# Cross-attention of a fused decoder layer: order of the probability scaling, steps that make the keys, slot of the context split

## The reference, cut to what matters

```python
x = _layernorm(x + _L0_attn_ref(x, ...))
x = _layernorm(x + _L0_xattn_ref(x, ctx_1024, ctx_1024, Wq, Wk, Wv, Wo))
x = _layernorm(x + _L0_ffn_ref(x, ...))
# _L0_xattn_ref: 32 sequences, 256 queries of width 256, 120 context rows, 16 heads of 64
q = jnp.einsum('bsd,dhk->bshk', query_input, Wq)
k = jnp.einsum('bsd,dhk->bshk', key_input, Wk)
v = jnp.einsum('bsd,dhk->bshk', value_input, Wv)
logits = jnp.einsum('bthk,bfhk->bhft', k, q * depth ** (-0.5))
ctx = jnp.einsum('bhft,bthk->bfhk', jax.nn.softmax(logits, axis=-1), v)
return jnp.einsum('bfhk,hkd->bfd', ctx, Wo)
```

## Time and profile before

| what | value |
|---|---|
| median of 3 runs | 3204.7 us |
| profiled execution | 3207.9 us |
| its span | 3206.2 us |
| cross-attention, first to last `shift` (L1275, 256 steps) | 1218.6 to 2302.8 us of the span |
| busy in 1300 to 2253 us (953 us): PE, PEld, DVE, ACT, POOL | 909.05, 861.73, 850.67, 836.25, 586.65 us |

### The profile page before, as it was taken

One profiled execution on the slowest core, in us unless ns is written; L12 is line 12 of the kernel. 1 busy time (PEld: TensorE's weight loads), 2 busy tenths in 40 slices (PEclk: granted clock), 3 DMA queues, 4 the chain that ended last, 5 costly groups with the idle time before them and its releaser, 6 DMA issues. The chain is left out here.

```text
span 3206.2 us, 79485 instructions
## 1 busy us (share of the span) xinstructions
PE 3067.2 (96%) x22112; PEld 2854.9 (89%) x22112; DVE 2376.3 (74%) x6822; ACT 2245.6 (70%) x7186; POOL 1874.9 (58%) x3414
## 2 busy tenths in 40 slices
PE   6999999999999988999999999999779999999998
PEld 5999999999999988998999988899768888889998
DVE  5787777777877777888889889898745455554565
ACT  6888888888887777888888888888734444442222
POOL 3666767666776766666666656666636666653000
PEclk8999999999999999999999999999889999999999
DMA  6444444444444440211111111111234444433333
GB/s 179 116 124 126 125 123 123 120 121 125 110 122 120 120 126 24 64 44 54 54 45 53 57 44 60 48 48 57 81 109 112 107 97 100 111 73 80 124 124 105
DMA packets 193705, 300.82 MB, mean 94 GB/s; under 512 B 33856, under 2 KB 134080, under 8 KB 192704
## 3 DMA queue, kind: packets, MB, share of 16 engines
q1 hardware_dynamic: 168768, 262.91, 27.7%
q0 software_dynamic: 24576, 33.57, 6.2%
HBM read 116.02 MB, written 67.11 MB: 57 GB/s over the span
## 5 line engine op out<-in xcount | busy, mean ns | idle before, releaser
L973 POOL TENSOR_SCALAR ca_prob<-ca_prob,ca_inverse 128x120 f32<-128x120 f32 x1024 | 360.5, 371 | 221.8 <-DVE ca_inverse L1281 219.5
L665 ACT ACTIVATE sa_prob<-sa_prob,sa_shift 128x128 f32<-128x128 f32 (+1 forms) x1024 | 453.7, 461 | 2.6 <-DVE sa_shift L718 2.6
L1218 ACT ACTIVATE ca_prob<-bank,ca_shift 128x120 f32<-128x120 f32 x1024 | 353.9, 362 | 18.8 <-DVE ca_shift L1275 17.4
L460 POOL TENSOR_SCALAR sa_prob<-sa_prob,sa_inverse 128x128 f32<-128x128 f32 x512 | 200.2, 391 | 231.0 <-DVE sa_inverse L726 217.1
L718 DVE CUSTOM_DVE_ANT_0 sa_prob<-bank,sa_mask 128x128 f32<-128x128 f32 (+1 forms) x1024 | 304.6, 352 | 6.2 <-PE bank L138 2.2
L136 PE MATMUL bank<-sa_ow,sa_y_hi 128*128 128x256 f32 x1024 | 278.8, 303 | 0.0
L136 PE MATMUL bank<-sa_kvT_a,sa_q 128*128 128x128 f32 (+1 forms) x1024 | 250.6, 280 | 18.1 <-DMA sa_q<-sa_q_tile 17.6
L138 PE MATMUL bank<-sa_kvT_b,sa_q 112*128 112x128 f32 (+1 forms) x1024 | 261.1, 280 | 0.0
L749 DVE TENSOR_TENSOR sa_pT_lo<-bank,sa_pT_hi 128x384 fp32r<-128x384 f32 x512 | 258.3, 544 | 1.5 <-ACT sa_pT_hi L650 1.4
L138 PE MATMUL bank<-sa_ow,sa_y_lo 112*128 112x256 f32 x1024 | 258.0, 282 | 0.0
L1694 POOL DMA_INDIRECT mid_acc<-ex_out,ex_to_tokens x112 | 191.0, 1705 | 105.4 <-DVE ex_out L1956 73.1
(11 more groups left out here) (257 smaller groups left out, 12179.8 us busy)
## 6 DMA issues: line engine op xcount, KB each, us to landing
sa_q<-sa_q_tile SPq DMA_DIRECT2D x128, 288.0 KB
sa_q<-sa_q_tile SPq DMA_DIRECT2D x160, 112.0 KB
mid_x2T<-ca_x2T SPq DMA_DIRECT2D x32, 512.0 KB
ex_sx<-mid_x2T SPq DMA_DIRECT2D x32, 512.0 KB
sa_q<-sa_q_tile SPq DMA_DIRECT2D x304, 32.0 KB, 2.0
sa_xT_raw<-in_xT SPq DMA_DIRECT2D x32, 256.0 KB, 2.9
sa_q<-sa_q_tile SPq DMA_DIRECT2D x32, 256.0 KB
sa_x_res<-in_x SPq DMA_DIRECT2D x32, 256.0 KB
```

What stands on the lines that cost most here:

```text
L460: pool.tensor_scalar(prob[:, r, hh, 0:P], prob[:, r, hh, 0:P], inverse[:, r, 2 * hh:2 * hh + 1], 1.0, ALU.mult, ALU.mult)
L665: act.activation(prob[:, r, hh, cols], prob[:, r, hh, cols], ACT.Exp, bias=shift[:, r, n:n + 1], scale=-1.0, accum_out=total[:, r, n:n + 1 ...
L973: ins = pool.tensor_scalar(prob[:, r, t, hh], prob[:, r, t, hh], inverse[:, r, n:n + 1], 1.0, ALU.mult, ALU.mult)
L1218: act.activation(prob[:, r, t, hh], SC[g % 2][:, n * S:n * S + S], ACT.Exp, bias=shift[:, r, n:n + 1], accum_out=total[:, r, n:n + 1]).the ...
```

## The change

Three edits, all in the cross-attention.

1. On GpSimd the scaling of step m-5 comes before the context split of step m-9.
2. The keys of pair pr are no longer made in its steps 0 to 7 but in the steps K_AT = -4, -3, -1, 0, 2, 3, 5, 6 counted from its first, so in slots 14 and 15 of the pair before and 1, 2, 4, 5, 7, 8 of its own. Pair 0 keeps steps 0 to 7. Functions `k_step`, `k_at` and `keys_by` say which key a step makes and how many are made by then; TensorE now waits in every slot until the keys so far have been read from the shared bank.
3. The context tile of a pair is split four slots ahead (CT_AT = -4, slot 12 of the pair before).

The loop over bodies ends one body earlier; body 7 is written out, since its last steps make no keys. The words "halved value products" answer to no line of the diff: the four matmuls of lines 1088 and 1089 are as they were.

```diff
+    def k_step(J, pr, p):
+        return p if isinstance(J, int) and J == 0 and pr == 0 else pr * 2 * NP + K_AT[p]
+    def pairs_near(J, g):
+        return [pr for pr in range(g // (2 * NP), g // (2 * NP) + 2)
+                if pr >= 0 and (not isinstance(J, int) or J * (SEQS // 2) + pr < B // 2)]
+    def k_at(J, g):
+        return next(((pr, p) for pr in pairs_near(J, g) for p in range(NP) if k_step(J, pr, p) == g), None)
+    def keys_by(J, g):
+        done = sum(k_step(J, pr, p) <= g for pr in range(4) for p in range(NP) if not isinstance(J, int) or J * (SEQS // 2) + pr < B // 2)
+        return J * (SEQS // 2 * NP) + done
+    def pair_at(J, m):
+        at = 0 if isinstance(J, int) and J == 0 and m == 0 else CT_AT
+        pr = (m - at) // (2 * NP)
+        here = (m - at) % (2 * NP) == 0 and seq_exists(J, 2 * pr) and not (isinstance(J, int) and J == 0 and pr == 0 and m != 0)
+        return pr if here else None
...
+    K_AT, CT_AT = (-4, -3, -1, 0, 2, 3, 5, 6), -4
...
 gpsimd:
-            g = m - CL - 1
-            (c_hi, c_lo)
             g = m - IL
             (prob by inverse, four operations)
+            g = m - CL - 1
+            (c_hi, c_lo)
...
 tensor:
-                if b == 1 and p == 0:
-                    need(pe, klo_done, upto_pair(J, g // (2 * NP), NP))
-                if b == 0:
-                    need(pe, clo_done, upto_pair(J, g // (2 * NP)))
-                    need(pe, klo_done, upto_pair(J, g // (2 * NP), NP, p + 1 - qk_before(J, g) - NP))
+                need(pe, klo_done, keys_by(J, g - qk_before(J, g)))
+                if k_at(J, g) is not None:
+                    pr, of = k_at(J, g)
+                    wk = slice(of * P, of * P + P)
+                    need(pe, clo_done, upto_pair(J, pr))
...
 scalar, vector (context):
-            if m % (2 * NP) == 0 and seq_exists(J, m // NP):
+            pr = pair_at(J, m)
+            if pr is not None:
...
 scalar, vector (keys):
-                if b == 0:
+                if k_at(J, g) is not None:
...
-    over_bodies(eng, ca_body, ca_first, BODIES, BODIES, begin=1)
+    over_bodies(eng, ca_body, ca_first, BODIES - 1, BODIES, begin=1)
```

More of the change, by code:

```diff
@@ L975, in slot @@
                 ins.then_inc(p_done, 1)
+            g = m - CL - 1
+            if step_exists(J, g):
+                r = g % RING
+                need(pool, o_mm, upto(J, g - RING))
+                need_alone(pool, csum_done, upto(J, g), spare_pool)
+                pool.tensor_scalar(c_hi[:, r], c[:, r], 1.0, 1.0, ALU.mult, ALU.mult).then_inc(cxhi_done, 1)
+                need_alone(pool, cxhi_done, upto(J, g), spare_pool)
+                pool.tensor_tensor(c_lo[:, r], c[:, r], f32(c_hi[:, r]), ALU.subtract).then_inc(cxlo_done, 1)
             if m % NP == NORM % NP and seq_exists(J, (m - NORM) // NP):
@@ L1064, in slot @@
                 ws = slice(p * P, p * P + P)
-                if b == 1 and p == 0:
-                    need(pe, klo_done, upto_pair(J, g // (2 * NP), NP))
-                if b == 0:
-                    need(pe, clo_done, upto_pair(J, g // (2 * NP)))
-                    need(pe, klo_done, upto_pair(J, g // (2 * NP), NP, p + 1 - qk_before(J, g) - NP))
+                need(pe, klo_done, keys_by(J, g - qk_before(J, g)))
[3 more added lines that the diff above has]
+                    need(pe, clo_done, upto_pair(J, pr))
                     for k in range(KC):
-                        mm = three(pe, K, w["wk"][0][:, k, ws], w["wk"][1][:, k, ws],
+                        mm = three(pe, K, w["wk"][0][:, k, wk], w["wk"][1][:, k, wk],
                                    cT_hi[:, k].rearrange("p b s -> p (b s)"), cT_lo[:, k].rearrange("p b s -> p (b s)"),
@@ L1139, in slot @@
         def slot(J, m):
-            if m % (2 * NP) == 0 and seq_exists(J, m // NP):
-                pr = m // (2 * NP)
+            pr = pair_at(J, m)
+            if pr is not None:
                 need(act, c_in, upto_pair(J, pr, 32))
@@ L1175, in slot @@
                 act.activation(q_hi[:, r], qk_bank(J, g)[:, 0:T], ACT.Copy).then_inc(qhi_done, 1)
-                if b == 0:
-                    need(act, k_mm, upto_pair(J, g // (2 * NP), NP, p + 1 - NP))
-                    need(act, s_mm, upto(J, g - NP))
+                if k_at(J, g) is not None:
+                    pr, of = k_at(J, g)
+                    need(act, k_mm, keys_by(J, g))
+                    need(act, s_mm, upto(J, pr * 2 * NP - NP + of))
                     for hh in range(2):
                         rows = slice(hh * DH, hh * DH + DH)
-                        ins = act.activation(k_hi[rows, :, p, hh * S:hh * S + S],
+                        ins = act.activation(k_hi[rows, :, of, hh * S:hh * S + S],
                                              qk_bank(J, g)[rows, T:T + 2 * S].rearrange("k (b s) -> k b s", b=2), ACT.Copy)
@@ L1240, in slot @@
         def slot(J, m):
-            if m % (2 * NP) == 0 and seq_exists(J, m // NP):
-                need(dve, chi_done, upto_pair(J, m // (2 * NP)))
+            pr = pair_at(J, m)
+            if pr is not None:
+                need(dve, chi_done, upto_pair(J, pr))
                 dve.tensor_tensor(cT_lo[:], cT_raw[:], f32(cT_hi[:]), ALU.subtract).then_inc(clo_done, 1)
@@ L1285, in slot @@
                 need(dve, qhi_done, upto(J, g))
-                if b == 0:
-                    need(dve, khi_done, upto_pair(J, g // (2 * NP), NP, p + 1 - NP))
+                if k_at(J, g) is not None:
+                    need(dve, khi_done, keys_by(J, g))
                 dve.tensor_tensor(q_lo[:, r], qk_bank(J, g)[:, 0:T], f32(q_hi[:, r]), ALU.subtract).then_inc(qlo_done, 1)
-                if b == 0:
+                if k_at(J, g) is not None:
+                    _, of = k_at(J, g)
                     for hh in range(2):
-                        at = (slice(hh * DH, hh * DH + DH), slice(None), p, slice(hh * S, hh * S + S))
+                        at = (slice(hh * DH, hh * DH + DH), slice(None), of, slice(hh * S, hh * S + S))
                         ins = dve.tensor_tensor(k_lo[at], qk_bank(J, g)[hh * DH:hh * DH + DH, T:T + 2 * S].rearrange("k (b s) -> k b s", b=2),
```

## The result

The changed kernel takes 3214.9 us (median of 8 runs, 3213.0 to 3217.8), the kernel before on the same chip 3204.1 us (8 runs): a ratio of 1.0033, 95% interval 1.0022 to 1.0044. It is slower by 0.3%, where 3188 us and a gain were forecast, and it lies just above the range. The profiled execution took 3215.3 us.

What follows compares the result with a forecast made beforehand. TensorE, VectorE and ScalarE were taken to bound the stage, the pacing engine changing by zone. Per pair A +0.2, B -1.34, C 0 gave -1.1 us, -17 us over 15 pairs: 3188 us, range 3152 to 3213.

Steps and rivals of the forecast that it cites:

- zone C: Slots 10 to 13 of a pair, where VectorE, and behind it GpSimd, hold PE; forecast change 0.
- PE's 0.8 us: Slot 12: with scaling first, PE's output products start near 1656.75 us instead of 1657.59, 0.8 us earlier.
- absorbed: Slots 10 and 1: later `c_lo` makes output products wait 0.5 us each; costed at nothing, as VectorE stops PE again.
- zone A: Slots 14 to 4 of the next pair, where VectorE sets the pace, busy 25.1 of 27 us.
- -0.57 in A: Context split: `cT_lo` leaves slot 0, taking 0.57 us a pair off VectorE, which sets the pace there.
- +0.57 in C: Context split: `cT_lo` comes to slot 12, 0.57 us more on VectorE, already at 10.45 of 11 us.
- rival 4: Slot 12: `cT_lo` and `c_lo` meet on SBUF, up to 0.65 us a pair, 3197 us; chance 0.20 together with rival 3.
- A +0.8: Slots 14 to 4: two net key steps cost VectorE +1.62 us, less 0.8 for filled waits and the `k_hi` ring.
- B -1.34: Zone B, slots 5 to 9, where PE sets the pace: loses two key steps, -1.34 us a pair.
- rival 3: Zone A: `k_lo` in slots 14 and 15 fills no gap, +1.62 us, 3199 us; chance 0.20 together with rival 4.
- Queue at nothing: Context tile's load on SyncE: issued more than a slot of eight before its split, so costed at nothing.
- Jump at nothing: Loop's end: body 7 written out, the loop jumps back once less; costed at nothing.

Runs made afterwards that it cites:

- e6: Kernel before with all cross-attention bodies written out, no hardware loop: 3198.9 us, ratio 0.9984.
- e7: e1 with all bodies written out, no hardware loop: 3195.3 us, ratio 0.9974.
- e1: Kernel before with edit 1 alone, GpSimd's scaling before the context split: 3197.5 us, ratio 0.9988.
- e8: e4 with all bodies written out (scaling first, split in slot 12, early load, keys in own steps 0 to 7): 3199.0 us, ratio 0.9983.
- e2: Changed kernel with edit 1 taken back, context split before scaling on GpSimd: 3232.6 us, ratio 1.0100.
- e17: e5 with VectorE's context split moved behind the maximum, still in slot 12: 3196.7 us, ratio 0.9971.
- e5: e3 with all bodies written out, no hardware loop: 3201.2 us, ratio 0.9991 to the kernel before.
- e3: Changed kernel with pair 1's context tile loaded one sequence earlier on SyncE: 3203.9 us, ratio 1.0006 to the kernel before.
- e4: e3 with the keys back in steps 0 to 7 of their own pair, hardware loop kept: 3213.4 us, ratio 1.0036.
- e9: e8 with key step 0 moved to slot 13 of the pair before: 3184.9 us, ratio 0.9940.
- e10: e8 with key steps 0 and 1 moved to slots 13 and 14 of the pair before: 3196.4 us, ratio 0.9977.
- e14: e9 with the hardware loop kept: 3211.3 us, ratio 1.0012 to the kernel before.

## Why the prediction was wrong, step by step

- **Edit 1, the scaling.** Forecast 0 in zone C because `cT_lo` would take up PE's 0.8 us, and both 0.5 us waits for `c_lo` absorbed. Alone (e6 to e7) it gives C -0.73 and A +0.37. The 0.8 us was right; "absorbed" was not: the waits for `c_lo` came 39 times in e1, 25 of them within zone A. That they are the 0.37 us is likely, but no run took them away alone.
- **Edit 3, the context split.** Forecast -0.57 in A; e7 to e8 gives -0.52. Forecast +0.57 in C; measured +0.65. Edits 1 and 3 together leave C at -0.08 (e6 to e8), where I had 0. That is right by the number and partly by luck: some 0.5 us of the +0.65 is the meeting with `c_lo`, which I had as rival 4 with 0.65 us at most and a small chance. It was there in 14 of the 15 pairs whose split had moved. My mark for it, GpSimd's splits over 0.9 us, did not show it: they took 0.86 to 0.88 us, and VectorE paid. The Trainium skill's rule (SBUF — State Buffer, Who interferes with whom), that a VectorE instruction with two SBUF inputs and a GpSimd instruction that reads SBUF shut each other out, holds here with 1.18 us instead of 0.66; which of the two waits is not always the one drawn second, for in e2 GpSimd's scalings start 0.11 us ahead of `cT_lo` and take 0.91 us instead of 0.37, while `cT_lo` keeps its 0.65. Without the meeting zone C would have had a gain (e17: 13.68 against 14.28 in e6).
- **Edit 2, the keys: the term that was mis-sized.** Forecast A +0.8, B -1.34. Measured (e8 to e5) A +1.61, B -1.59. Two net key steps cost VectorE's full price in A: the +1.62 of the working, of which I took off 0.8 for gaps that they would fill. In sum they filled none: VectorE's waits in zone A add to 2.2 us a pair in e8 and 2.3 in e5. The gap at the values did shrink in slot 1, from 1.0 to 0.5 us (before written out, e6, has 0.5 there too), but the waits for `k_hi` in zone A grew from 0.4 to 1.5 us, where I had taken 0.3 off for them. Over all slots that wait did not halve but went from 23.7 to 42.2 us, in e5 to 42.3. The steps of slots 14 and 15, 1 and 2, 4 and 5, 7 and 8 still follow each other. That is rival 3. What the edit wins in B it loses in A, +0.03 us.
- **The steady sum.** Forecast -1.1 us a pair. Written out, the three edits give 67.78 - 67.99 = -0.21: 0.9 us a pair, 13 us, of the miss of 27 us. With the loop it is +0.17.
- **"Queue at nothing": the step that failed outright.** I named what a late tile would do (ScalarE and all behind it would stand) and did not read when pair 1's load was issued. It was in the trace of before: 1255.6 us, 9.5 us ahead of the split at 1265.1, while the split moved ahead by 13 us (to 1252.1 in e3). It costs 8.7 us by the ratios (e3). Of the +11.0 us in the profile's first 16 steps it is 6.4 (76.2 to 69.8); 3.4 more are pair 1's keys (69.7 in e5, 66.3 in e8), of which the last 11 steps give back 0.9. Most of the 10.8 us that the change loses is this one load.
- **"Jump at nothing".** Wrong twice, with opposite signs. The exit's stall left the end (-7.2 us there, 5.9 of them the exit's by e6), and jumps that before rode over cost the kernel after four gaps of 2.4 to 2.9 us and a stretch at a lower clock. The two about cancel: by the ratios the loop costs 5 us in before and 5 in e3. So the number 0 came out near the truth by luck.
- **The marks that I set.** PE's wait for `ca_prob` under 3 us: yes. `cT_lo` wait gone: yes. `c_lo` waits once a pair: yes, 15 times, but 0.2 us each and not 0.5 (one of 1.5). The steps' mean at 4.18 us: no, 4.28. `ca_res` stays: no, it went. It stands in slot 10, right behind the key step that left slot 9: in e8, whose keys stay in slots 2 to 9, it is 8.5 us as in before, and in e5 it is gone. I had not counted that edit 2 would take it. The `shift` intervals in slots 14 to 1 over 0.5 us longer: slots 14 and 1 are (6.10 us from 4.90, 5.89 from 4.30), and that was my mark for rival 3. Nothing outside the stage by over 1 us: 1.3, on both sides of it together, in one execution of each kernel.

The range ended at 3213 us and failed by 2: it was made of costs per pair alone, with nothing for events that happen once.

Left open: why the jump stops PE for 0.7 us at most in before and for 3.4 in e4, and why the clock fell behind some stops and not behind others as long. Taking away the wait of the query products for `k_lo` was not tried, since both use the same bank; it is in e8, whose zone B is that of e7 (23.17 and 23.19 us), so there it costs nothing. The forecast and the result differ by 27 us: the tile's 8.7 and the steady sum's 13 are measured, and no single run separates the remaining 5.

## What to carry to other kernels

Before moving an operation ahead in a pipeline, find the issue time of its input in the first round, not in the steady one, and write the once-only costs as terms of their own. In this kernel one step was worth moving out of the slot where several of the pacing engine's extras meet (e9); spreading work evenly paid nothing, since the other slots' engine was as full (e5, e10). Waits by name can halve with no gain: measure from start to start of one instruction that stands in every step.

## What the runs showed of the hardware that I had not expected

- A jump of the hardware loop stopped PE for up to 3.5 us (e14), and behind each of e4's and e14's five stops, but behind only one of the kernel after's four, some microseconds ran at 1.2 GHz (0.53 in e4's window of 6 us). The same loop cost from 5 us (before) to 23 us (e14 against e9) of the program.
- VectorE's subtraction of two SBUF tiles, 128 x 480, took 1.18 us instead of 0.66 when it started 0.20 us behind GpSimd's subtraction of two SBUF tiles (0.86 instead of 0.74). Started 0.07 us ahead of it, it took 0.65 and GpSimd's 1.16 (e5).
